# Moving small jobs from GpSimd to VectorE and SyncE inside a mixture-of-experts loop, with part of the loop unrolled

## The chip, the cores and the metric

One Trainium2 chip, one of its cores. The metric is the device time of one execution in microseconds (us); lower is better. The kernel before was run three times: 969.45, 964.38 and 969.40 us, median 969.4 us.

Engine names in the profile: PE is TensorE (PEld its weight loads), DVE is VectorE, ACT is ScalarE, POOL is GpSimd, SP is SyncE, which here only issues DMAs.

## The reference

One transformer block over x of 4 x 512 tokens and 512 channels, in float32: a modulation by a condition vector, an RWKV-style attention part (five 512 x 512 products), a channel mix (512 to 2048 and back), and then the part that matters here, a mixture of experts:

```python
probs = jax.nn.softmax(xt @ W_router, axis=-1)
top_v, top_i = jax.lax.top_k(probs, K_TOP)          # 2 of 16 experts per token
sh_mid = gelu(xt @ Wsh_up); shared_out = sh_mid @ Wsh_down
rt_mid = gelu(xt @ Wrt_up[e]);  routed_out = sum of gate * (rt_mid @ Wrt_down[e])
x = x + gb * (shared_out + routed_out)
```

Each token goes through the shared expert (512 to 512 to 512) and through two of the 16 routed experts (512 to 256 to 512).

## The kernel before, in words

Every float32 operand of a large product is split into a high and a low part, and a product is three matmuls (`mm3`, lines 417 to 421: high x high, high x low, low x high). The split of a tile is a copy (high part) and a subtraction (low part).

The order of the work of each engine is written out by hand, one program per engine, with semaphores between them. After the channel mix the kernel has these stages:

1. Shared expert for batches 0 and 1 (`shared_up`, `shared_down`, tiles of 128 tokens numbered t = 0 to 7). `gb_shared(t)` on DVE (L1737) multiplies the result in PSUM by a modulation row, into `base8[:, t]`, and raises `s_gsh`. Its PSUM banks are used again by the routed experts.
2. Scatter of the tokens to expert order in HBM (`xs_s`, by GpSimd's indirect DMA), with a table that says which expert each tile of 128 rows belongs to.
3. The expert loop: 41 tiles here, two per iteration (`pair`), in a hardware loop over `pairs` on each of PE, DVE, ACT and SP. Per tile: SP loads 128 rows (`load_xs`), PE transposes them (`turn_x`, L1174), ACT writes the high part of `xsT` (L2236), DVE the low part (`turned_lo`, L1841, which reads PSUM and `xsT`), PE multiplies by the expert's first matrix (`up`), ACT applies GELU (L2240), PE transposes that (`turn_m`, L1207), ACT and DVE split it (L2244, L1846), PE multiplies by the second matrix (`down`), DVE copies the result to SBUF (`y_out`, L1854), SP stores it (`store_y`).
4. The shared expert for batches 2 and 3, while GpSimd gathers the routed results and DVE combines them; then the output is stored.

Beside stage 3 GpSimd makes the weights ready: for experts 4 to 15 it loads half an expert (0.5 MB) into `stage` (`expert_load`, L2424) and splits it (`expert_split`: L2442 the high part, L2444 the low part; both read SBUF operands and write SBUF). The split weights stand in a ring of 5 slots; `expert_done` (L2427) makes GpSimd wait until PE has finished the expert that held the slot. PE waits for an expert on `s_exr` before `up` (L1189).

After the two halves of expert 4 (n = 0 and 1), GpSimd stops splitting and does other jobs (L2480 to L2486): six DMA loads of `x4` tiles (`x4_load`, L2453), the low part of the activations of batch 2 (`ht_lo(2)`, L2403, 4 subtractions of 128 x 512), eight additions `base8 + x4` (`base_add`, L2459, 128 x 512 each), and four DMA loads of the activations of batch 3 (`last_ht_load`, L2466). Then it goes on with expert 5.

PE's order around the start of stage 3 is L1161 to L1232: down tile 4 and 5, `turn_x(0)`, down tile 6, `up(0)`, `turn_x(1)`, down tile 7, `turn_m(0)`, with waits on `s_gsh` for 6, 7 and 8 in between, and then the loop.

Of the kernel before, what the change touches and what calls it, by code (L numbers as in the profile page):

```python
# [36 lines left out]
RING = 7  # L37
BASE = 2
PRE = 4
AHEAD = 2  # L40
SB = 2
ERING = RING - BASE
# [21 lines left out]
def adaln_block(nc, x_d, c_d, wmod_d, vecs_d, wtm_d, wcm_d, wrt_d, wex_d, out_d):  # L64
    top = ExitStack()
    with top:
        def sem(name):
            return top.enter_context(nc.semaphore(name))
# [258 lines left out]
        s_base = sem("s_base")  # L327
        s_gb = sem("s_gb")
        s_x4l = sem("s_x4l")
        s_x4p = sem("s_x4p")  # L330
        s_htp = sem("s_htp")
        s_sub = sem("s_sub")
        s_exp = sem("s_exp")
        s_gates = sem("s_gates")
# [124 lines left out]
        def x4_of(t):  # L459

            return x4m[:, t] if t < 2 else x4r[:, t - 2]
# [89 lines left out]
        def _(sp):  # L551
# [186 lines left out]
            def load_ht(b):  # L738
                for i in range(2):
                    sp.wait_ge(s_h5Tst[i], 32 * (b + 1))  # L740
                if b == 0:
                    sp.wait_ge(s_kk, (NB - 1) * MF + 12)
                elif b == 1:
                    sp.wait_ge(s_kvt, TT)
                else:
                    sp.wait_ge(s_up, KT)
                for k in range(KT):
                    sp.dma_start(ht_of(b)[:, 1, k].bitcast(F32), h5T_s[b, :, k, :]).then_inc(s_h5r[b % 2], 16)

# [11 lines left out]
            def load_x4(tiles):  # L761
                for t in tiles:
                    sp.wait_ge(s_x4st[t % TT], 16 * (t // TT + 1))
                    if t == 0:
                        sp.wait_ge(s_xklo, NB * KT)
                    sp.dma_start(x4_of(t), x4_s[t]).then_inc(s_x4l, 16)

            def scatters_landed(b):
# [52 lines left out]
            def load_xs(q, par, wait=None):  # L821
                tile = tile_of(q)
                if wait is not None:
                    sp.wait_ge(s_tx, wait)
                sp.dma_start(xsb[:, par], rows(xs_s, tile)).then_inc(s_xs[par], 16)
# [7 lines left out]
            load_xs(1, 1)  # L833
            load_xs(2, 0, 1)
            load_xs(3, 1, 2)
            def pair(i):
                load_xs(i * 2 + 4, 0, i * 2 + 3)
                store_y(i * 2, 0, i * 2 + 1 + AHEAD)
                load_xs(i * 2 + 5, 1, i * 2 + 4)
                store_y(i * 2 + 1, 1, i * 2 + 2 + AHEAD)  # L840

            pairs = sp.value_load(tend[0:1, NE:NE + 1], min_val=NE // 2, max_val=NS // 2)
            with sp.Fori(0, pairs) as i:
                pair(i)
            store_y(pairs * 2, 0, pairs * 2 + 1 + AHEAD)
            sp.wait_ge(s_yst[0], pairs * 16 + 32)
# [9 lines left out]
        def _(pe):  # L856
# [304 lines left out]
            shared_down(1, [0], first)  # L1161
            table_row()
            shared_down(1, [0], rest)
            shared_down(1, [1], every)
            pe.wait_ge(s_tab, 1)

            def turn_x(q, par, xs_count, free_count):

# [8 lines left out]
            def word_of(q):  # L1177

                return nc.values_load(tab[0:1, 0, bass.ds(q, 1)], engines=[mybir.EngineType.PE], min_val=0,
                                      max_val=8 * NE - 1,  # L1180
                                      skip_runtime_bounds_check_because="a word is 9 e + BASE - ERING (e // ERING), e under NE")

            def slot_of(word):

                return nc.s_assert_within(
                    word & 7, 0, RING - 1, skip_runtime_bounds_check_because="the low bits are (.. mod RING)")
# [33 lines left out]
                mm.then_inc(s_d4, 1)  # L1220

            turn_x(0, 0, 16, None)
            shared_down(1, [2], every)
            w0 = word_of(0)
            w1 = word_of(1)
            pe.wait_ge(s_gsh, SB * TT - 2)
            up(w0, slot_of(w0), 0, 1, None)
            turn_x(1, 1, 16, None)
            shared_down(1, [3], every)
            pe.wait_ge(s_gsh, SB * TT - 1)  # L1230
            turn_m(0, 0, 1, None)
            pe.wait_ge(s_gsh, SB * TT)  # L1232

            def pair(i, w0, w1):
                up(w1, slot_of(w1), 1, i * 2 + 2, i * 2 + 1)
# [29 lines left out]
        def _(dve):  # L1265
# [445 lines left out]
                    place_c(b - 1)  # L1711

            def ht_lo(b, tiles):
                if 0 in tiles:
                    dve.wait_ge(s_htlo, b * KT)
                hi, lo = (ht_of(b)[:, i] for i in range(2))
                for k in tiles:
                    dve.wait_ge(s_hthi, b * KT + k + 1)
                    dve.tensor_tensor(lo[:, k, :], lo[:, k, :].bitcast(F32), hi[:, k, :].bitcast(F32), ALU.subtract)\
                        .then_inc(s_htlo, 1)  # L1720
# [7 lines left out]
            def gb_shared(t):  # L1728
                dve.wait_ge(s_dn, t + 1)
                dve.wait_ge(s_gb, 16 * (t // TT + 1))  # L1730
                if t < TT:
                    dve.wait_ge(s_x4st[t], 16 * NB)
                if t == TT:
                    dve.wait_ge(s_rt, NT)
                    for i in range(2):
                        dve.wait_ge(s_h5Tst[i], 16 * NT // 2)
                dve.tensor_tensor(base8[:, t], dn_ps[t % 4][:, :], gb_bc[:, :], ALU.mult).then_inc(s_gsh, 1)  # L1737

            def gates_a():

# [90 lines left out]
            mid_lo(6)  # L1831
            mid_lo(7)
            table_d()
            gates_b()
            gb_shared(TT)
            gb_shared(TT + 1)


            def turned_lo(par, count):
# [17 lines left out]
            dve.sem_inc(s_yst[1], 16)  # L1857
            dve.sem_inc(s_yst[0], 16)
            turned_lo(0, 1)
            gb_shared(TT + 2)  # L1860
            turned_lo(1, 2)
            gb_shared(TT + 3)
            turned_mid_lo(0, 1)
            pairs = dve.value_load(tend[0:1, NE:NE + 1], min_val=NE // 2, max_val=NS // 2)

# [5 lines left out]
                y_out(1, i * 2 + 2, i * 16 + 16)  # L1871
                turned_mid_lo(0, i * 2 + 3)

            with dve.Fori(0, pairs) as i:
                pair(i)
            y_out(0, pairs * 2 + 1, pairs * 16 + 16)

# [12 lines left out]
            def combine_b(t):  # L1890
                b = t // TT
                if t >= SB * TT:
                    dve.wait_ge(s_gsh, t + 1)
                dve.wait_ge(s_bsl, 16 * (NT - SB * TT + NB))
                if t == 0:
                    dve.wait_ge(s_base, SB * TT)
                base = base8[:, t] if t < SB * TT else bsb[:, t - SB * TT]
                done(dve.tensor_tensor(g1b[:, t], g1b[:, t], gb2[:, b], ALU.mult))
                dve.tensor_tensor(g1b[:, t], g1b[:, t], base, ALU.add).then_inc(s_o4, 1)
# [24 lines left out]
        def _(act):  # L1924
# [239 lines left out]
                act.activation(h5T_of(t), t5_ps[:, :, :], ACT.Copy).then_inc(s_h5T, 1)  # L2164

            def ht_hi(b, tiles=range(KT)):
                if b == NB - 1:
                    act.wait_ge(s_htp, 64)
                    act.wait_ge(s_end, 2)
                else:  # L2170
                    act.wait_ge(s_h5r[b % 2], 64 * (b // 2 + 1))
                for k in tiles:
                    act.activation(ht_of(b)[:, 0, k, :], ht_of(b)[:, 1, k, :].bitcast(F32), ACT.Copy)\
                        .then_inc(s_hthi, 1)
# [109 lines left out]
        def _(pool):  # L2284
# [110 lines left out]


            def ht_lo(b, tiles=range(KT)):
                if b:
                    pool.wait_ge(s_htlo, b * KT)
                for k in tiles:  # L2400
                    n = b * KT + k
                    pool.wait_ge(s_hthi, n + 1)
                    pool.tensor_tensor(ht[:, 1, k, :], ht[:, 1, k, :].bitcast(F32), ht[:, 0, k, :].bitcast(F32),  # L2403
                                       ALU.subtract).then_inc(s_htlo, 1)
# [41 lines left out]
                    pool.wait_ge(s_exd, 2 * n + 2)  # L2446
                    pool.sem_inc(s_exr, 8)

            def x4_load(t):
                pool.wait_ge(s_x4st[t % TT], 16 * (t // TT + 1))  # L2450
                if t == 2:
                    pool.wait_ge(s_dn, SB * TT)
                pool.dma_start(x4_of(t), x4_s[t]).then_inc(s_x4p, 16)  # L2453

            def base_add(t):
                pool.wait_ge(s_gsh, t + 1)
                pool.wait_ge(s_x4l, 16 * 2)
                pool.wait_ge(s_x4p, 16 * (SB * TT - 2))
                pool.tensor_tensor(base8[:, t], base8[:, t], x4_of(t), ALU.add).then_inc(s_base, 1)  # L2459

            def last_ht_load():
                pool.wait_ge(s_base, SB * TT)
                for i in range(2):
                    pool.wait_ge(s_h5Tst[i], 16 * NT // 2)
                for k in range(KT):
                    pool.dma_start(ht_of(NB - 1)[:, 1, k].bitcast(F32), h5T_s[NB - 1, :, k, :])\  # L2466
                        .then_inc(s_htp, 16)

            halves = 2 * (NE - PRE)
            pool.wait_ge(s_wlo, 38)  # L2470
            expert_load(0)
# [4 lines left out]
            for n in range(halves):  # L2476
                expert_split(n)
                if n + 2 < halves:
                    expert_load(n + 2)
                if n == 1:  # L2480
                    for t in range(2, SB * TT):
                        x4_load(t)
                    ht_lo(2)
                    for t in range(SB * TT):
                        base_add(t)
                    last_ht_load()  # L2486

                if n == 16:
                    pool.wait_ge(s_gates, 1)
                    for b in range(NB):  # L2490
                        pool.dma_start(gb2[:, b], mod_s[5, b:b + 1, :].partition_broadcast(P)).then_inc(s_bsl, 16)
# [57 lines left out]
```

## Time and profile before

| what | value |
|---|---|
| median of three executions | 969.4 us |
| the profiled execution's own time | 969.45 us |
| its span (first to last instruction) | 967.7 us |
| PE busy | 896.3 us, 93% |
| DVE busy | 537.9 us, 56% |
| POOL busy | 399.2 us, 41% |
| stage 3 (from the first `up` of the loop to the last `down`) | about 747.6 to 908 us |

The shares are averages over stages with different limits. The profile's views used here are the page itself, the timeline of single engines in a stretch, tables of stretches, the listing of a tile, and the chain that ended last.

### The profile page before, as it was taken

To read this page: it belongs to the slowest core of one execution; us is meant where nothing else is said; L and a number is where in the kernel's file an instruction comes from. 1 tells how busy PE (TensorE), PEld (TensorE's weight loads), DVE (VectorE), ACT (ScalarE), POOL (GpSimd) and SP (SyncE) were. 2 spreads that over 40 slices of the span, in tenths; PEclk is the share of its full clock that TensorE was granted. 3 is DMA by queue.
4 is the path that set the end of the run, shared out by engine and by line. 5 is a ranking of instruction groups with operands and counts; after the bars stand their busy time and mean duration, and the time that the engine had idled before them with its cause. 6 is when DMAs were issued, how large, how long until landed. Compare 5 with 4: busy or idle time off the path is not lost.

```text
span 967.7 us, 13687 instructions
## 1 busy us (share of the span) xinstructions
PE 896.3 (93%) x4264; PEld 722.9 (75%) x4265; DVE 537.9 (56%) x983; ACT 383.8 (40%) x632; POOL 399.2 (41%) x314
## 2 busy tenths in 40 slices
PE   7898879999998999999999899989997999989993
PEld 2457658878776788887888788878876888878782
DVE  5896998987657111355144514451772444444488
ACT  2566455573735542321232122225441333333441
POOL 2322200100022437236104600469337989889273
PEclk9898979999998999999999999999999999999997
DMA  9549477566054536144115301564545777786686
GB/s 358 181 132 278 143 226 253 163 197 205 1 186 146 168 99 202 49 157 148 44 54 172 122 33 55 191 226 159 164 144 152 231 239 232 236 264 201 210 262 206
DMA packets 106720, 166.69 MB, mean 172 GB/s; under 512 B 8344, under 2 KB 53400, under 8 KB 105136
## 3 DMA queue, kind: packets, MB, share of 16 engines
q1 hardware_dynamic: 59184, 112.07, 34.4%
q0 software_dynamic: 10336, 35.13, 11.5%
q10 hardware_dynamic: 37152, 18.88, 6.6%
q8 instruction: 27, 0.44, 0.2%
q14 instruction: 21, 0.17, 0.1%
HBM read 98.63 MB, written 67.42 MB: 172 GB/s over the span
## 4 chain that ended last, share of the span: by engine, by line
PE 60%; POOL 14%; DVE 13%; issue 5%; DMA 4%; ACT 3%; POOLq 1%; SPq 0%; DVEq 0%; ACTq 0%
PE kv_ps L419 6%; PE kv_ps L421 6%; PE kv_ps L420 6%; PE kk_ps L419 6%; PE kk_ps L421 6%; PE kk_ps L420 6%; POOL ex_w L2444 5%; PE mm_ps L419 4%; PE mm_ps L420 4%; PE mm_ps L421 4%; POOL ex_w L2442 4%; DVE raw_ps L1352 2%; PE up_ps L419 2%; PE mm_ps L860 1%; DVE mix L1358 1%
## 5 line engine op out<-in xcount | busy, mean ns | idle before, releaser
L1552 DVE TENSOR_TENSOR silu<-kk_ps,silu 128x512 fp32r<-128x512 f32 x64 | 44.3, 692 | 205.2 <-ACT silu L2155 204.9
L2151 ACT ACTIVATE kk_ps<-kk_ps 128x512 f32<-128x512 f32 x64 | 37.2, 582 | 210.4 <-PE kk_ps L421 210.3
L419 PE MATMUL kk_ps<-xk,cm_w 128*128 128x512 f32 x256 | 101.0, 394 | 0.4 <-DVE silu L1552 0.4
L419 PE MATMUL kv_ps<-cm_w,silu 128*128 128x512 f32 x256 | 100.6, 393 | 0.0
L421 PE MATMUL kk_ps<-xk,cm_w 128*128 128x512 f32 x256 | 99.8, 390 | 0.0
L421 PE MATMUL kv_ps<-cm_w,silu 128*128 128x512 f32 x256 | 99.7, 390 | 0.0
L420 PE MATMUL kk_ps<-xk,cm_w 128*128 128x512 f32 x256 | 99.7, 389 | 0.0
L420 PE MATMUL kv_ps<-cm_w,silu 128*128 128x512 f32 x256 | 99.6, 389 | 0.0
L2327 POOL TENSOR_TENSOR rs<-mv,neghalf 128x4 f32<-128x4 f32 x12 | 13.6, 1133 | 162.7 <-DVE mv L1281 162.6
L1841 DVE TENSOR_TENSOR xsT<-xs_ps,xsT 128x512 fp32r<-128x512 f32 x42 | 29.1, 692 | 90.9 <-ACT xsT L2236 90.9
L2320 POOL TENSOR_TENSOR cm_w<-stage,cm_w 128x1024 fp32r<-128x1024 f32 x16 | 38.7, 2425 | 91.8 <-ACT cm_w L1942 91.8
L2372 POOL TENSOR_TENSOR rs<-mv,neghalf 128x1 f32<-128x1 f32 x16 | 16.2, 1015 | 137.6 <-DVE mv L1577 137.6
L1970 ACT ACTIVATE mix<-raw_ps 128x512 fp32r<-128x512 f32 x64 | 37.4, 596 | 64.0 <-DVE raw_ps L1352 57.6
L419 PE MATMUL mm_ps<-mix,wkv_w 128*128 128x512 f32 x128 | 54.7, 428 | 7.9 <-DVE x2b L1391 4.4
L419 PE MATMUL up_ps<-ex_w,xsT 128*128 x164 | 50.2, 306 | 9.4 <-issue 6.2
L2444 POOL TENSOR_TENSOR ex_w<-stage,ex_w 128x1024 fp32r<-128x1024 f32 x24 | 57.4, 2390 | 1.9
L419 PEld LDWEIGHTS kk_ps<-xk,cm_w 128*128 128x128 f32 x256 | 48.1, 188 | 10.6 <-DVE silu L1552 0.8
L421 PEld LDWEIGHTS kk_ps<-xk,cm_w 128*128 128x128 f32 x256 | 48.1, 188 | 10.2
L421 PEld LDWEIGHTS kv_ps<-cm_w,silu 128*128 128x128 f32 x256 | 48.0, 188 | 10.1
L420 PEld LDWEIGHTS kv_ps<-cm_w,silu 128*128 128x128 f32 x256 | 48.1, 188 | 9.8
L419 PEld LDWEIGHTS kv_ps<-cm_w,silu 128*128 128x128 f32 x256 | 48.1, 188 | 9.8
L420 PEld LDWEIGHTS kk_ps<-xk,cm_w 128*128 128x128 f32 x256 | 48.1, 188 | 9.6
(275 smaller groups left out, 2368.4 us busy)
## 6 DMA issues: line engine op xcount, KB each, us to landing
xs_s<-zero ACTq DMA_DIRECT2D x13, 1024.0 KB, 6.0
stage<-in_wex POOLq DMA_DIRECT2D x24, 512.0 KB, 5.0
xsb<-xs_s SPq DMA_DIRECT2D x44, 256.0 KB, 3.5
ys_s<-ysb SPq DMA_DIRECT2D x41, 256.0 KB, 2.8
stage<-in_wcm SPq DMA_DIRECT2D x16, 512.0 KB, 3.8
wmod<-in_wmod SPq DMA_DIRECT2D x6, 1024.0 KB, 11.7
ex_raw<-in_wex SPq DMA_DIRECT2D x6, 1024.0 KB, 7.5
stage<-in_wtm SPq DMA_DIRECT2D x10, 512.0 KB, 6.2
```

The source lines that it names most:

```text
L419: pe.matmul(out, lhs[0], rhs[0], start=first, stop=False)
L420: pe.matmul(out, lhs[0], rhs[1], start=False, stop=False)
L421: return pe.matmul(out, lhs[1], rhs[0], start=False, stop=last)
L1352: dve.scalar_tensor_tensor(out=out, in0=dT[:, k, :], scalar=vecs[:, vec, k:k + 1], in1=hT[:, k, 0:T], op0=ALU.mult, op1=ALU.add).then_inc( ...
L1552: dve.tensor_tensor(silu[:, g % NSILU, 1, :], kk_ps[g % 2][:, :], silu[:, g % NSILU, 0, :].bitcast(F32), ALU.subtract).then_inc(s_silo, 1)
L1841: dve.tensor_tensor(xsT[:, par, 1], xs_ps[par][:, :, :], xsT[:, par, 0].bitcast(F32), ALU.subtract)\
L1970: act.activation(mix[:, i % 2, 0, k, :], raw_at(s, b, k), ACT.Copy)\
L2151: act.activation(kk_ps[g % 2][:, :], kk_ps[g % 2][:, :], ACT.Silu).then_inc(s_silu, 1)
L2320: pool.tensor_tensor(w[:, 1, k0:k0 + KT // 2, :], stage[:, n % 2].rearrange("p (k c) -> p k c", c=H), w[:, 0, k0:k0 + KT // 2, :].bitcast( ...
L2372: pool.tensor_tensor(rs5[:, t % 2:t % 2 + 1], mv5[:, t % 2, 1:2], neghalf[:, :], ALU.pow)\
L2442: pool.tensor_tensor(hi, stage[:, n % 2], zero[:, 0:1].to_broadcast([P, HALF]), ALU.add).then_inc(s_exd, 1)
L2444: pool.tensor_tensor(lo, stage[:, n % 2], hi.bitcast(F32), ALU.subtract).then_inc(s_exd, 1)
```

## The change

The four jobs leave GpSimd. The six `x4` loads and the four loads for batch 3 are issued by SP. `ht_lo(2)`, the eight `base_add` and `gates_b` (three small operations that stood before the loop) go to DVE, spread over the first seven pairs: after pair 0 and 1 two subtractions each, after pairs 2 to 5 two additions each, after pair 6 `gates_b`. For that, the first seven iterations are written out on DVE and on SP, and the hardware loop there starts at 7; PE's and ACT's loops stay as they are. On PE, down tiles 6 and 7 now stand before `turn_x(0)`, with a single wait for `s_gsh` 8.

```diff
+PEEL = 7
 # SP
                 elif b == 2:
+                    sp.wait_ge(s_up, KT)
                 else:
-                    sp.wait_ge(s_up, KT)
+                    sp.wait_ge(s_dn, SB * TT)
                 for k in range(KT):
                     sp.dma_start(ht_of(b)[:, 1, k].bitcast(F32), h5T_s[b, :, k, :]).then_inc(s_h5r[b % 2], 16)
...
+                    if t == 2:
+                        sp.wait_ge(s_dn, SB * TT)
                     sp.dma_start(x4_of(t), x4_s[t]).then_inc(s_x4l, 16)
...
             load_xs(3, 1, 2)
+            load_x4(range(2, SB * TT))
...
+            for i in range(PEEL):
+                pair(i)
+            sp.wait_ge(s_base, SB * TT)
+            load_ht(NB - 1)
             pairs = sp.value_load(tend[0:1, NE:NE + 1], min_val=NE // 2, max_val=NS // 2)
-            with sp.Fori(0, pairs) as i:
+            with sp.Fori(PEEL, pairs) as i:
 # PE
-            shared_down(1, [1], every)
+            shared_down(1, [1, 2, 3], every)
             pe.wait_ge(s_tab, 1)
+            pe.wait_ge(s_gsh, SB * TT)
...
             turn_x(0, 0, 16, None)
-            shared_down(1, [2], every)
             w0 = word_of(0)
+            up(w0, slot_of(w0), 0, 1, None)
             w1 = word_of(1)
-            pe.wait_ge(s_gsh, SB * TT - 2)
-            up(w0, slot_of(w0), 0, 1, None)
             turn_x(1, 1, 16, None)
-            shared_down(1, [3], every)
-            pe.wait_ge(s_gsh, SB * TT - 1)
             turn_m(0, 0, 1, None)
-            pe.wait_ge(s_gsh, SB * TT)
 # DVE
+            def base_add(t):
+                dve.wait_ge(s_gsh, t + 1)
+                dve.wait_ge(s_x4l, 16 * SB * TT)
+                dve.tensor_tensor(base8[:, t], base8[:, t], x4_of(t), ALU.add).then_inc(s_base, 1)
...
-            gates_b()
...
-            with dve.Fori(0, pairs) as i:
+            def beside(i):
+                if i < 2:
+                    ht_lo(2, [2 * i, 2 * i + 1])
+                elif i < 6:
+                    base_add(2 * i - 4)
+                    base_add(2 * i - 3)
+                else:
+                    gates_b()
+
+            for i in range(PEEL):
+                pair(i)
+                beside(i)
+            with dve.Fori(PEEL, pairs) as i:
                 pair(i)
 # GpSimd
-                if n == 1:
-                    for t in range(2, SB * TT):
-                        x4_load(t)
-                    ht_lo(2)
-                    for t in range(SB * TT):
-                        base_add(t)
-                    last_ht_load()
```

## Rows read from the trace of the kernel before

**Rows 1.** The page, part 4: engines' shares of the chain that ended last.
```profile
PE 60%; POOL 14%; DVE 13%; issue 5%; DMA 4%; ACT 3%; POOLq 1%; SPq 0%; DVEq 0%; ACTq 0%
```

**Rows 2.** Table of stretches: start:end, length, busy us per engine, PEclk, DMA share, GB/s.
```profile
770.00:868.00 98.00, 94.69 (x605) 80.69 (x603) 43.97 (x77) 34.24 (x75) 87.23 (x57) 1.00 0.75 242
...
752.00:757.00 5.00, 4.65 (x34) 4.11 (x33) 2.03 (x4) 1.37 (x3) 3.90 (x4) 1.00 1.01 386
```

**Rows 3.** Timeline of PE before the loop: start, length, engine, operation, [idle before].
```profile
737.26 0.63 PE L1174 MATMUL xs_ps<-ident,xsb 128*128 128x128 f32 x4 [3.06 <-DMA xsb<-xs_s]
...
740.23 0.39 PE L421 MATMUL dn_ps<-ex_w,mid 128*128 128x512 f32 x1
...
745.08 0.38 PE L1207 MATMUL tm_ps<-ident,mb 128*128 128x128 f32 x2
747.60 0.38 PE L419 MATMUL up_ps<-ex_w,xsT 128*128 x1 [2.13 <-issue]
```

**Rows 4.** Timeline of DVE there: `gb_shared` of tiles 6 and 7.
```profile
740.66 0.69 DVE L1737 TENSOR_TENSOR base<-dn_ps,gb_bc 128x512 f32<-128x512 f32 x1 [1.41 <-PE dn_ps L421]
...
745.28 0.69 DVE L1737 TENSOR_TENSOR base<-dn_ps,gb_bc 128x512 f32<-128x512 f32 x1 [1.43 <-PE dn_ps L421]
```

**Rows 5.** PE's waits from 748 to 904 us; its timeline, and POOL's, at the longest.
```profile
PE up_ps L419 <- POOLq L2447: 2.3, 1, 2.3
...
870.38 0.38 PE L419 MATMUL up_ps<-ex_w,xsT 128*128 x1 [2.34 <-POOLq L2447]
...
867.55 2.34 POOL L2444 TENSOR_TENSOR ex_w<-stage,ex_w 128x1024 fp32r<-128x1024 f32 x1
```

**Rows 6.** Timeline of POOL: the jobs that move, experts 5 and 15.
```profile
747.64 3.23 POOL L2453 DMA_DIRECT2D x4r<-x_s  x6
...
770.13 1.89 POOL L2442 TENSOR_TENSOR ex_w<-stage,zero 128x1024 fp32r<-128x1024 f32 x1 [0.21 <-issue]
...
881.94 1.90 POOL L2442 TENSOR_TENSOR ex_w<-stage,zero 128x1024 fp32r<-128x1024 f32 x1
```

**Rows 7.** One pair's turn: DVE's and PE's timelines, L1841's durations (ns, min/median/max).
```profile
755.62 0.42 DVE L1846 TENSOR_TENSOR mbT<-tm_ps,mbT 128x256 fp32r<-128x256 f32 x1
758.33 0.69 DVE L1841 TENSOR_TENSOR xsT<-xs_ps,xsT 128x512 fp32r<-128x512 f32 x1 [2.29 <-ACT xsT L2236]
...
757.06 0.60 PE L1174 MATMUL xs_ps<-ident,xsb 128*128 128x128 f32 x4
759.32 0.38 PE L419 MATMUL up_ps<-ex_w,xsT 128*128 x1
...
L1841 DVE TENSOR_TENSOR xsT<-xs_ps,xsT x39: 691/692/693, 750.4 to 900.4; 128x512 fp32r<-128x512 f32 x39
```

**Rows 8.** Earlier stage, timelines of DVE and POOL: operations side by side.
```profile
630.77 1.10 DVE L1617 TENSOR_TENSOR lg<-lg,rev 128x64 f32<-128x64 f32 x1
631.91 0.22 DVE L1618 TENSOR_REDUCE top<-lg 128x4 f32<-128x64 f32 x1
632.16 0.96 DVE L1619 TENSOR_TENSOR oh<-rev,top 128x64 f32<-128x64 f32 x1
...
684.32 2.73 DVE L1568 TENSOR_TENSOR x4b<-x4b,ub 128x512 f32<-128x512 f32 x1
689.51 0.69 DVE L1568 TENSOR_TENSOR x4b<-x4b,ub 128x512 f32<-128x512 f32 x1
...
630.50 1.29 POOL L2353 TENSOR_TENSOR x4b<-x4b,bc 128x512 f32<-128x512 f32 x1 [0.74 <-DMA h5b<-in_x]
631.75 1.29 POOL L2354 TENSOR_TENSOR ub<-ub,bc 128x512 f32<-128x512 f32 x1
...
681.76 4.75 POOL L2314 TENSOR_TENSOR ex_w<-ex_raw,ex_w 128x1024 fp32r<-128x1024 f32 x2 [3.92 <-ACT ex_w L1931]
```

**Rows 9.** SP's DMA issues, and issue to landing of `xsb` (748 to 904 us).
```profile
700.73 2.56 SPq L748 DMA_DIRECT2D ht<-h5T_s  x4
...
DMA to landing us min/median/max: 2.5/3.3/6.7
```

More of the change, by code:

```diff
@@ L329, in adaln_block @@
         s_x4l = sem("s_x4l")
-        s_x4p = sem("s_x4p")
-        s_htp = sem("s_htp")
         s_sub = sem("s_sub")
@@ L744, in load_ht @@
                     sp.wait_ge(s_kvt, TT)
+                elif b == 2:
+                    sp.wait_ge(s_up, KT)
                 else:
-                    sp.wait_ge(s_up, KT)
+                    sp.wait_ge(s_dn, SB * TT)
                 for k in range(KT):
@@ L1713, in ht_lo @@
             def ht_lo(b, tiles):
-                if 0 in tiles:
-                    dve.wait_ge(s_htlo, b * KT)
+                if b == 1 and 0 in tiles:
+                    dve.wait_ge(s_htlo, KT)
                 hi, lo = (ht_of(b)[:, i] for i in range(2))
@@ L1833, in _ @@
             table_d()
-            gates_b()
-            gb_shared(TT)
-            gb_shared(TT + 1)
+            for t in range(TT, SB * TT):
+                gb_shared(t)
             def turned_lo(par, count):
@@ L1859, in _ @@
             turned_lo(0, 1)
-            gb_shared(TT + 2)
             turned_lo(1, 2)
-            gb_shared(TT + 3)
             turned_mid_lo(0, 1)
@@ L1894, in combine_b @@
                 dve.wait_ge(s_bsl, 16 * (NT - SB * TT + NB))
-                if t == 0:
-                    dve.wait_ge(s_base, SB * TT)
                 base = base8[:, t] if t < SB * TT else bsb[:, t - SB * TT]
@@ L2166, in ht_hi @@
             def ht_hi(b, tiles=range(KT)):
+                act.wait_ge(s_h5r[b % 2], 64 * (b // 2 + 1))
                 if b == NB - 1:
-                    act.wait_ge(s_htp, 64)
                     act.wait_ge(s_end, 2)
-                else:
-                    act.wait_ge(s_h5r[b % 2], 64 * (b // 2 + 1))
                 for k in tiles:
@@ L2397, in ht_lo @@
             def ht_lo(b, tiles=range(KT)):
-                if b:
-                    pool.wait_ge(s_htlo, b * KT)
                 for k in tiles:
@@ L2447, in expert_split @@
                     pool.sem_inc(s_exr, 8)
[L2449 to L2467, printed above, removed]
             halves = 2 * (NE - PRE)
```

## The prediction

> **What bounds the kernel now.** I read the page's chain first [rows 1]: PE holds 60% of it and POOL 14%. The reader is to see that POOL is on the chain at all, since it computes nothing of the output directly; most of its share lies in the expert loop. So next comes the table of stretches over the loop [rows 2]: between 770 and 868 us PE is busy 94.69 of 98 us and POOL 87.23 of 98. Both run close to full, PE a little more. Then PE's waits in the loop [rows 5]: one of 2.34 us at 870.38, released by POOL's count of finished experts, because the second half of that expert's split began at 867.55 and took 2.34 us. Last the hand-over into the loop: PE waits 3.06 us for the first rows [rows 3], and stands 2.13 us idle before the `up` at 747.60. A tile of the loop takes PE (870.38 - 2.34 - 747.60) / 31 = 3.89 us [rows 3, 5]: from the `up` of tile 1 to that of tile 32 are 31 tiles. (Tile 0's `up` stands before the loop; an iteration begins with the `up` of an odd tile, and the stalled one is in the middle of the sixteenth.) A pair is 7.77 us.
>
> The profiled execution took 969.45 us, 1.75 more than its span, and is the upper one of the three, 0.05 above the median of 969.4. I sum against it.
>
> **Part 1, POOL freed.** POOL leaves splitting at 747.64 and comes back at 770.13 [rows 6]: 22.5 us for 6 DMA issues, 12 tensor operations and 4 DMA issues. All go. Not all 22.5 us are gained: expert 5 takes the slot of expert 0, so its split waits until PE has finished expert 0, which has two or three tiles (41 tiles over 16 experts). The last `down` of tile q ends about 3.4 us after the `up` of tile q+1 (3.89 less the half microsecond of `turn_m`), so with the loop entered at 746.6 (below) expert 0 is done at about 754 or 758, and POOL is 12 to 16 us earlier than 770.13. From there it needs (881.94 - 770.13) / 10 = 11.2 us per expert [rows 6] against PE's 3.89 x 41 / 16 = 10.0, so it falls back about 1.2 us per expert, as before, and reaches expert 13 still 12 us early or more. The stall of 2.34 us goes. What is late next is nothing of POOL's: later experts had no wait before either. Term: -2.34, bounds 0 and -2.34.
>
> **Part 2, the hand-over.** Before, two `down` tiles lie behind `turn_x(0)`. Now they fill the 3.06 us in which PE waited for the first rows. PE is free at 737.26 - 3.06 = 734.20. A tile is 12 matmuls, about 2.75 us, so both are done at about 739.7. The new wait for all eight of `s_gsh` stands before `turn_x(0)`: DVE multiplies tile 7 in 0.69 us [rows 4], it started 0.04 us after the last matmul of tile 6 ended (740.23 + 0.39), so about 740.45, and PE starts `turn_x(0)` at about 740.6. Behind that wait is the whole of PE's queue and through it ACT, DVE and SP's loads. From a `turn_x` to the next `up` over ACT and DVE are 759.32 - 757.06 = 2.26 us [rows 7]: `up(0)` at 742.9, itself 3.89 - 2.26 = 1.6 us, `turn_x(1)` at 744.5. Now this chain is exposed a second time, with nothing but `turn_m(0)` under it: `up(1)` at 744.5 + 2.1 = 746.6. Before it was 747.60. There, PE's last wait ended with DVE's multiply at 745.28 + 0.69 = 745.97 [rows 4], so entering the loop took it 1.6 us; now `turn_m(0)` can go at about 745.1 and the entry ends by 746.7, so both ways agree. Term: -1.0. Bounds: a gain of 2.1 (all the idle before 747.60), a loss of 0.5 (the reads of expert words that stood under a `down` tile are now bare).
>
> **Part 3, the work put on DVE.** By time alone it is free. At a pair's end DVE stands idle 2.29 us before the next L1841 [rows 7], and two operations of 128 x 512 take about 1.3 us (0.69 each, the second starting a little into the first). But L1841 has hardly any room behind it: it ends at 759.02 and PE's `up` starts at 759.32. A DVE that comes out of its extra work more than about 2.3 us after the pair's end holds PE, microsecond for microsecond.
>
> The rows that matter are from another stage [rows 8]. L1617 (both inputs in SBUF, 128 x 64) took 1.10 us, while the single-input L1618 beside it took 0.22. POOL was in an operation from 630.50 to 631.79, and L1617 ended at 631.87, just after it. L1619, again two SBUF inputs, came at 632.16 into the next POOL operation (631.75 to 633.04) and ended at 633.12. In the wide form it is the same: L1568 took 2.73 us at 684.32, where the identical one at 689.51 took 0.69; POOL was in two splits from 681.76 to 686.51. So a DVE operation with two SBUF inputs waits for POOL's running operation to end. L1841 never does: 39 of it at 691 to 693 ns with POOL busy nine tenths of the time [rows 7, 2]; one of its inputs is PSUM. The operations that the change brings into the loop, `ht_lo` and `base_add`, have both inputs in SBUF, and on POOL they could not meet a split, since they ran in its own order.
>
> The Trainium skill says the same as a rule, against this change ("SBUF — State Buffer", on the engines' shared port pair): a VectorE instruction with two SBUF inputs contends with a GpSimd instruction that reads SBUF, and whichever comes second is blocked for the whole of the first. By the rule the price is the one below, while a reader who goes by durations alone would put this part at zero; the trace agrees with the rule, 2.73 us against 0.69.
>
> The price: half an expert is one POOL operation of 1.9 us, one of 2.35 us directly after it, and about 1.3 us of idle and issuing (5.6 in all). The first DVE operation falls into the 1.9 (34%): it waits 0.95 on average, runs 0.69, then POOL's next is first in line for 2.35, then the second DVE operation 0.69; together 4.7, which is 2.4 over the 2.3 that are free. Into the 2.35 (42%): the wait is up to 2.35 and then both run, 1.3 to 3.7, on average 0.4 over. Into the rest (24%): half of the time the second operation meets the next 1.9, 0.9 over. Mean 0.34 x 2.4 + 0.42 x 0.4 + 0.24 x 0.45 = 1.1 us per pair. Pairs 0 to 5 have two such operations each; at the end of pair 0, about 755, POOL may still wait for expert 0. Five pairs give 5.4. Bounds: 0, and 6 x 3.3 = 20 for the worst phase each time. I take +5.4, since the rows show blocking wherever such operations met. `gates_b` after pair 6 has one operation of the kind, a small one: +0.2 (0 to 1). POOL is held by the same lock, 0.7 us each time, which its lead of 12 us hides.
>
> **Part 4, the work put on SP.** Ten issues move into SP's queue. At 700.73 four took 2.56 us [rows 9], 0.64 each. The six `x4` loads, behind `load_xs(3)` at about 745.2, take 3.8 us and push `load_xs(4)` from about 748.9 to 749.9; it is needed by `turn_x(4)`, 757.06 before, 756.0 now, and landing takes 3.3 us, at most 6.7 [rows 9]. That maximum is this very load, when the same 1.5 MB came from POOL's queue and the DMA engines were full, 386 GB/s at share 1.01 [rows 2]. The bytes are the same and come 2 us sooner, so I expect no stall. Behind pair 6, SP does four loads (2.56), a register read and the loop's entry, then `load_xs(18)`: some 3 us late, with 4 us of room at the median landing and 1 MB queued ahead: +0.3. Together 0 to 3; I take +0.3. Landing of the batch 3 data itself is not late: it is needed after 910.
>
> Gone from the hand-over are also `gates_b` on DVE (under PE's tile 5, worth nothing). The stage after the loop waits for the last store and shifts as a whole.
>
> **Sum.** 969.45 - 2.34 - 1.0 + 5.4 + 0.2 + 0.3 = 972.0 us, 2.6 over the median before.
>
> **Rivals.** (a) The blocking costs nothing, because the operations fall into POOL's idle parts or PE's own waits cover it: 969.45 - 3.3 + 0.3 = 966.4. For it: POOL is idle or issuing a quarter of the time, and at pair 0 perhaps waiting. Against: rows 8, and six chances. (b) The other side, slower than before: the pair's end falls into POOL's 1.9 us operation in most pairs, 2.4 us each. POOL's half of 5.6 and the pair of 7.8 drift against each other, but a PE that is held moves with POOL. Five at 2.4 make 12 instead of 5.4: about 979. It shows as slower from a total of 8.2 us of blocking on (3.3 gained, 4.9 of tolerance). (c) SP's bursts: `turn_x(4)` and `turn_x(18)` wait 1 to 3 us for their rows, together 3 more than in my sum: 975. For it, the landing of 6.7 us with only about 0.5 to spare; against it, no wait for rows in the whole loop before. (d) The stall moves instead of vanishing would give 974.3, but needs 12 us of lead lost; I give it nothing of its own.
>
> **How the numbers follow.** Main case 0.52, (a) 0.22, (b) 0.13, (c) 0.13. Within 0.5% (4.9 us either way, about what a measurement of this kernel tells from no change; one of its three runs was 5 us below the others) lie 0.38 of the main case, whose own range is 968 to 978, 0.14 of (a) and 0.06 of (c): 0.58. Slower: 0.13 + 0.13 + 0.07 = 0.33 (main above 974.3, all of (b), half of (c)). Faster: the rest of (a) with a low draw like 964.38, 0.08, and a little for unknown gains, 0.09. The range 965 to 979 leaves out the low draws and the far end of (b).
>
> **What would show it.** PE's wait for L2447 gone, and POOL's expert 5 beginning at 754 to 758; the `up` of tile 1 at 746.6. L1719 and the new additions in the loop with maxima of 2.5 to 3 us instead of 0.69, and PE idle before the middle `up` of pairs 1 to 6, 0 to 3 us each, released by DVE's `xsT`. If these operations last 0.69 throughout, part 3 is wrong and (a) holds. If PE waits for `xsb`, (c). If POOL begins expert 5 later than 760, part 1's lead was smaller than I think.

## The result, and the profile after

The changed kernel took 974.6 us (median of 13 executions, 969.33 to 978.12), the kernel before 965.4 us (13, 963.05 to 970.13): ratio 1.0093, 95% interval [1.0077, 1.0110]. That is 9 us slower. Forecast were 972.0 us and a range of 965 to 979. The time lies inside, but the difference is the better measure: forecast +2.6 us over a before of 969.45, measured +9.2 between the medians. "Slower by over 0.5%" had a chance of 0.33 only. The profiled execution took 973.85 us, span 972.1 us, 4.4 over the span of before.

From the page of the changed kernel, the share of the chain that ended last, against [rows 1]:

```profile
PE 74%; DVE 15%; issue 4%; DMA 3%; ACT 2%; SPq 1%; DVEq 0%; ACTq 0%
```

POOL is gone from it, and yet the kernel is slower. Freeing an engine on the chain is worth only what PE waited for it, 2.34 us [rows 5]. The table of stretches, the first line against [rows 2]:

```profile
770.00:868.00 98.00, 90.80 (x569) 77.52 (x568) 54.47 (x83) 32.46 (x71) 82.78 (x53) 0.98 0.72 234
752.00:757.00 5.00, 4.81 (x33) 4.13 (x32) 3.77 (x5) 2.29 (x5) 2.94 (x2) 1.00 0.51 163
736.00:742.00 6.00, 3.38 (x17) 3.13 (x17) 1.38 (x2) 0.60 (x1) 5.60 (x4) 0.71 0.41 130
742.00:748.00 6.00, 4.62 (x22) 4.20 (x21) 1.02 (x2) 1.41 (x4) 1.42 (x2) 0.50 0.58 172
784.00:790.00 6.00, 3.96 (x19) 3.91 (x19) 2.68 (x4) 1.08 (x3) 5.44 (x4) 0.72 0.51 165
```

PE lost 3.9 us of work in the first stretch, and the granted clock (the third number from the end) is below 1.00 in the last three; the kernel before had 1.00 in all of them. PE's timeline in the loop, each row a first matmul of `up` with the idle time before it (the last row, tile 32, has none):

```profile
760.11 0.38 PE L418 MATMUL up_ps<-ex_w,xsT 128*128 x1 [2.06 <-issue]
...
764.04 0.38 PE L418 MATMUL up_ps<-ex_w,xsT 128*128 x1 [0.19 <-issue]
...
776.30 0.38 PE L418 MATMUL up_ps<-ex_w,xsT 128*128 x1 [0.73 <-issue]
...
786.05 0.39 PE L418 MATMUL up_ps<-ex_w,xsT 128*128 x1 [2.04 <-issue]
...
874.73 0.38 PE L418 MATMUL up_ps<-ex_w,xsT 128*128 x1
```

The 0.19 us is what every iteration's entry costs. The other three, with a second 0.73 at 803.70, stand after pairs 0, 2, 3 and 5: 5.56 us. The wait for POOL, 2.34 us at the same tile in [rows 5], has gone (last row). DVE's timeline names the cause of the four (operations that last too long), and POOL's beside it shows what they waited for. The two engines hold each other up; below this is called the lock. DVE first, then POOL:

```profile
754.90 4.31 DVE L1726 TENSOR_TENSOR ht<-ht 128x512 fp32r<-128x512 f32 x2
759.13 0.68 DVE L1852 TENSOR_TENSOR xsT<-xs_ps,xsT 128x512 fp32r<-128x512 f32 x1
...
764.64 1.28 DVE L1726 TENSOR_TENSOR ht<-ht 128x512 fp32r<-128x512 f32 x2
...
772.42 2.98 DVE L1749 TENSOR_TENSOR base<-base,x4m 128x512 f32<-128x512 f32 x2
...
780.84 4.31 DVE L1749 TENSOR_TENSOR base<-base,x4r 128x512 f32<-128x512 f32 x2
785.08 0.68 DVE L1852 TENSOR_TENSOR xsT<-xs_ps,xsT 128x512 fp32r<-128x512 f32 x1
...
792.15 1.28 DVE L1749 TENSOR_TENSOR base<-base,x4r 128x512 f32<-128x512 f32 x2
```

```profile
753.98 1.88 POOL L2458 TENSOR_TENSOR ex_w<-stage,zero 128x1024 fp32r<-128x1024 f32 x1 [9.97 <-PE dn_ps L420]
755.94 2.72 POOL L2460 TENSOR_TENSOR ex_w<-stage,ex_w 128x1024 fp32r<-128x1024 f32 x1
...
761.52 2.40 POOL L2460 TENSOR_TENSOR ex_w<-stage,ex_w 128x1024 fp32r<-128x1024 f32 x1
764.52 0.57 POOL L2440 DMA_DIRECT2D stage<-in_wex  x1 [0.60 <-POOL ex_w L2460]
767.67 1.88 POOL L2458 TENSOR_TENSOR ex_w<-stage,zero 128x1024 fp32r<-128x1024 f32 x1 [2.58 <-PE dn_ps L420]
...
772.91 1.94 POOL L2458 TENSOR_TENSOR ex_w<-stage,zero 128x1024 fp32r<-128x1024 f32 x1
774.93 2.71 POOL L2460 TENSOR_TENSOR ex_w<-stage,ex_w 128x1024 fp32r<-128x1024 f32 x1
...
790.43 0.57 POOL L2440 DMA_DIRECT2D stage<-in_wex  x1 [0.59 <-POOL ex_w L2460]
795.10 1.88 POOL L2458 TENSOR_TENSOR ex_w<-stage,zero 128x1024 fp32r<-128x1024 f32 x1 [4.10 <-PE dn_ps L420]
```

Two operations take 1.28 us when POOL stands still (at 764.64, where POOL issues a DMA and waits until 767.67; at 792.15, where it waits until 795.10) and 4.31 when they begin in one POOL operation and meet the next. At 754.90 the first waits until 755.86, the end of POOL's first operation, and runs. POOL's next is held by it (2.72 instead of 2.40), and the second DVE operation waits until 758.66. Then `xsT` starts at 759.13 and PE's `up` at 760.11, 2.06 us late. The 2.98 us at 772.42 (and 3.00 at 799.80) are the case between: the first operation begins just before POOL's and is through in 0.68, only the second waits, until 774.85, and PE loses 0.73. DVE's idle time does not show this; a reader of the totals sees an engine busy 57% of the span. The profile books PE's idle time to "issue", not to `xsT`; only the two timelines side by side show it.

The hand-over, against [rows 3] and [rows 4], on PE:

```profile
736.88 0.63 PE L1186 MATMUL xs_ps<-ident,xsb 128*128 128x128 f32 x4 [0.83 <-issue]
739.30 0.57 PE L418 MATMUL up_ps<-ex_w,xsT 128*128 x1 [1.79 <-DVE xsT L1852]
...
742.02 1.06 PE L1186 MATMUL xs_ps<-ident,xsb 128*128 128x128 f32 x4
742.87 0.63 PE L1219 MATMUL tm_ps<-ident,mb 128*128 128x128 f32 x2
744.88 0.58 PE L418 MATMUL up_ps<-ex_w,xsT 128*128 x1 [1.38 <-DVE xsT L1852]
...
747.61 1.05 PE L1186 MATMUL xs_ps<-ident,xsb 128*128 128x128 f32 x4
```

From an `up` to the next `turn_x` are 2.7 us here, and 1.5 before (`turn_x(2)` at 749.12, the `up` of [rows 3] at 747.60). `turn_x` itself shows 1.05 for 0.60. That is the clock of 0.50, the lower of its two levels (1.2 GHz).

To compare stretches I count from one event to another, since the profiles reach the expert table's transpose (`t_ps`) at different times; the differences before it, 3.6 us between these two, are in code that the change leaves alone. "Tile n" is the start of `turn_x(n)`:

| us | table to tile 2 | tile 2 to 18 | tile 18 to 41 | tile 41 to the end | sum |
|---|---|---|---|---|---|
| before | 18.9 | 62.2 | 91.6 | 64.8 | 237.5 |
| changed | 21.0 | 70.5 | 89.2 | 64.8 | 245.5 |

### The profile page after: what moved, and what is told of

Its sections match the earlier page's. It is cut to its first block, busy times and chain, and to the rows that moved or that the text cites. A ratio compares the mean times of both kernels' runs of the same rounds, so it can differ in the third digit from the quotient of the medians.

```text
span 972.1 us, 13587 instructions
## 1 busy us (share of the span) xinstructions
PE 897.2 (92%) x4264; PEld 724.7 (75%) x4265; DVE 553.9 (57%) x995; ACT 383.8 (39%) x632; POOL 379.7 (39%) x292
## 4 chain that ended last, share of the span: by engine, by line
PE 74%; DVE 15%; issue 4%; DMA 3%; ACT 2%; SPq 1%; DVEq 0%; ACTq 0%
PE kv_ps L418 6%; PE kk_ps L418 6%; PE kv_ps L420 6%; PE kk_ps L419 6%; PE kv_ps L419 6%; PE kk_ps L420 6%; PE mm_ps L418 4%; PE mm_ps L420 4%; PE mm_ps L419 4%; PE up_ps L418 4%; PE up_ps L419 3%; PE up_ps L420 3%; PE dn_ps L418 3%; PE dn_ps L420 3%; PE dn_ps L419 3%
```

## The experiments

In all variants PE's wait `s_exr >= word + 1` reads `(word & 127) + 1`, which has the same value and costs one register operation per tile. The variant c0_before measures that operation alone. There are three groups, each on a chip of its own with its own runs of before: e1 to e4 (before 970.35), then c1, e5 to e7 (973.06), then c0, c2, e8 (965.1). Ratios are to before unless said.

**e1_hand_back**: the changed kernel with the order of PE and DVE at the hand-over as before.

```diff
-            shared_down(1, [1, 2, 3], every)
+            shared_down(1, [1], every)
...
             turn_x(0, 0, 16, None)
+            shared_down(1, [2], every)
...
             turn_x(1, 1, 16, None)
+            shared_down(1, [3], every)
...
```

> The changed kernel with the hand-over into the loop put back as before on PE and DVE (down tiles 6 and 7 behind turn_x(0) and turn_x(1), the additions and loads stay on DVE and SP). Theory: of the 8.0 us that the loop's stretch grew, 2.1 lie before turn_x(2) and 0.45 in the tile after it at the lower clock; putting the order back takes them away: 974.6 - 2.5 = about 972. The granted clock should be 1.00 from 736 to 748 us, and the up of tile 1 take 1.5 us. Rival (my prediction's step): the new order was worth 1.0 us, so this gives about 975.6.

Measured 978.1 us, ratio 1.0071 [1.0044, 1.0097]. The same four stalls, at the same tiles: 2.06, 0.73, 2.06 and the small last. They do not hang on the hand-over. In its profile the clock is 1.00 from 736 to 748 and the table to tile 2 takes 18.2 us, as the theory has it. Its ratio is 3.5 us below that of c1_after and c2_after (1.0107 each), but those ran on other chips and the intervals overlap, so the gain of 2.5 us is not shown.

**e2_hand_only**: the kernel before with only that order new.

```diff
-            shared_down(1, [1], every)
+            shared_down(1, [1, 2, 3], every)
...
```

> The kernel before with nothing changed but that order on PE and DVE. Theory: turn_x(2) comes 2.5 us later, but PE then also comes later to expert 13, where it stood 2.3 us for GpSimd, so the loss is swallowed there: 965.4 + 0.2 = 965.6, with PE's wait for GpSimd near 0 and PEclk below 1.00 before the loop. Rival 1 (my prediction's step): a gain of 1.0, and the wait at expert 13 grows by it, so 965.4 too, but with turn_x(2) earlier. Rival 2: both add up, 968.

Measured 971.45 us, 1.0010 [0.9992, 1.0028]. The clock stayed at 1.00, and the table to tile 2 took 18.05 us, 0.8 less than before. PE then waits longer for POOL:

```profile
PE up_ps L419 <- POOLq L2443: 7.0, 3, 3.1
```

PE goes into the loop earlier and POOL does not, so what the hand-over gives comes back as waits for weights: 7.0 us in three, where before had 2.3. The wait did not fall to nothing, as the theory had it; rival 1 had its direction.

**e3_one_input**: the changed kernel, the twelve operations replaced by statistics of one 128 x 512 input (same length, one SBUF input; the sums and low parts are left out, so the output is not the reference's).

```diff
...
-                dve.tensor_tensor(base8[:, t], base8[:, t], x4_of(t), ALU.add).then_inc(s_base, 1)
+                dve.bn_stats(scrap[:, t], base8[:, t]).then_inc(s_base, 1)
```

> The changed kernel in which the four subtractions of batch 2 and the eight additions on DVE are replaced by statistics operations over the same 128 x 512 tile (one SBUF input, 0.69 us each in the trace of before); these results are left out. Theory (two SBUF inputs wait for GpSimd's running operation): each lasts 0.69, PE's idle before the middle up of pairs 1 to 6 goes, 5.4 us and 1.4 us of lower clock behind one of them: 974.6 - 6.8 = about 968. Rival (DVE's time, its waits or the written-out loop itself hold PE): 974.6, no change.

Measured 975.1 us, 1.0059 [1.0035, 1.0084]. From the grouped lines of DVE in the loop (line, operation, count, busy us, mean ns):

```profile
L1856 DVE TENSOR_TENSOR xsT<-xs_ps,xsT 128x512 fp32r<-128x512 f32 x39 | 27.0, 691 | 71.9 <-ACT xsT L2258 71.9
...
L1753 DVE BATCH_NORM_STATS2 scrap<-base 128x6 f32<-128x512 f32 x8 | 5.1, 680 | 0.0
L1766 DVE TENSOR_TENSOR gates<-pr,gates 128x16 f32<-128x16 f32 x1 | 2.0, 2030 | 0.0
```

680 ns, with POOL splitting as before: not one is held, while `gates_b`'s two-input operation over 128 x 16 took 2.03 us. All stalls in pairs 0 to 5 are gone (tile 2 to 18: 63.7 us instead of 70.5). So the lock is the second SBUF input, not DVE's time. Nor is it what they write, though the statistics write 6 columns and not 512: `xsT` writes 512 beside POOL and takes 0.691 us, with one input in PSUM, and `gates_b`, which writes 16, is held. The times do not show the gain. The profiled execution, 967.01 us, was the fastest of this variant's eight, and the median is 8 us above it; against e1_hand_back, which has the four stalls (and the old hand-over) and ran on the same chip, the mean is 2.4 us lower (e1 to e3 1.0025 [0.999, 1.006]). Where the other executions lost the 8 us, one profile does not tell.

**e4_loads_only**: the kernel before with only the ten DMA issues moved to SP.

```diff
+            load_x4(range(2, SB * TT))
...
+            sp.wait_ge(s_base, SB * TT)
+            load_ht(NB - 1)
```

> The kernel before in which only the ten DMA issues leave GpSimd for SP, placed as in the changed kernel; all arithmetic and the hand-over stay. Theory: GpSimd is about 7 us earlier at expert 5, the wait of 2.3 us at expert 13 goes, turn_x(18) waits about 1 us for its rows behind the four loads: 965.4 - 1.3 = 964.1. Rival: SP's bursts cost as much as the wait, 965.4 or more.

Measured 973.2 us, 1.0030 [1.0014, 1.0046], which is c0_before's ratio (below), so the ten issues by themselves are worth nothing that can be told; the forecast gain of 1.3 us did not come. The stall of expert 13 is gone, `turn_x(18)` is 1.0 us late, as in the changed kernel. The order of the hand-over is the old one, and yet the clock is 0.79 from 730 to 736 in its profile.

**c1_after**: the changed kernel, with the register operation.

> The changed kernel itself, once more, on the chip of the three others (only PE's wait for an expert takes its number from the low seven bits of the word, one register operation more per tile, as in all of these variants). It gives the base for them. Theory: ratio to before 1.009, the same four waits of PE in pairs 0, 2, 3 and 5 adding to 5.6 us, since the order of the engines is fixed. Whether PE's granted clock falls to 0.50 at 739 us again is open: if that fall comes from the new order, it must be there again and the tiles 1 and 2 take about 5 us each; if it is chance, the clock stands at 1.00 there in about half of the profiles and the hand-over is 2 to 3 us shorter.

Measured 983.4 us, 1.0107 [1.0082, 1.0131]. Stalls 1.98, 0.74 and two more at the same tiles. The clock stood at 1.00 throughout the hand-over:

```profile
742.88 0.38 PE L418 MATMUL up_ps<-ex_w,xsT 128*128 x1 [1.70 <-DVE xsT L1852]
...
746.82 0.38 PE L418 MATMUL up_ps<-ex_w,xsT 128*128 x1 [1.34 <-DVE xsT L1852]
```

The idle times before both `up` are nearly those of the changed kernel (1.79 and 1.38), and the `up` of tile 1 comes 16.5 us after the table instead of 18.2 (before: 17.4). So the clock does not follow from the new order: the same instructions met it at 1.00 here.

**e5_fill**: PE's idle time at the hand-over filled with transposes.

```diff
+            fill(5)
             turn_x(0, 0, 16, None)
+            fill(11)
...
             turn_m(0, 0, 1, None)
+            fill(8)
```

> The changed kernel with transposes of a constant put into PE's idle time before and behind turn_x(0) and behind turn_m(0) (5, 11 and 8 of 128 x 128, 0.15 us each, into unused columns of a PSUM bank; nothing reads them). Theory: the +2.1 us of the hand-over come from the lower granted clock after PE's idle time; with PE busy the clock stays at 1.00, up(0) and up(1) take 1.5 us instead of 2.9, and the time is 2 to 3 us below the changed kernel's (ratio to it 0.997). Rival 1, the reads of the expert words and the bare chain are the cost: nothing changes or the filler's own length adds 0.5 us. Rival 2, the clock falls by chance: it may fall here as well, at another place.

Measured 982.3 us, 1.0084 [1.0054, 1.0113]; against c1_after by the means of their runs 0.9986 [0.996, 1.001]. The clock stayed at 1.00, as it did in c1_after without filling, and the hand-over was 0.6 us longer (18.7). Whether filling helps in those executions in which the clock falls is not settled by this.

**e6_spread**: the changed kernel with one of the twelve operations after each half pair, instead of two after each pair.

```diff
                 turned_mid_lo(1, i * 2 + 2)
+                if between is not None:
+                    beside(between)
...
+            def beside(j):
+                if j < 4:
+                    ht_lo(2, [j])
+                elif j < 12:
+                    base_add(j - 4)
...
+                pair(i, 2 * i)
+                beside(2 * i + 1)
```

> The changed kernel with the twelve moved operations of DVE one by one, after every half pair, in place of two after each pair (same operations, same inputs, same count). Theory (blocking by POOL's running operation): a single operation waits at most 2.35 us and takes 0.69, which is 0.8 over the 2.2 us that are free, and mostly under it; so PE's waits of 5.6 us in pairs 0, 2, 3 and 5 fall to about 0.6 and the time is 5 us below the changed kernel's (ratio to before 1.004). Rival, that POOL's port blocks in any case and the cost goes with the number of such operations: 5.6 us stay. Rival, that the unrolled code or DVE's mere occupancy costs: the same 5.6 stay.

Measured 976.3 us, 1.0044 [1.0024, 1.0065]; against c1_after, on the same chip, 0.9938 [0.992, 0.996], 6 us, where 5 were forecast. The operations are still held, but singly (DVE's timeline; the third row is the `xsT` that PE waits for, the last is `gates_b`):

```profile
769.25 0.68 DVE L1749 TENSOR_TENSOR base<-base,x4m 128x512 f32<-128x512 f32 x1
...
773.19 1.84 DVE L1749 TENSOR_TENSOR base<-base,x4r 128x512 f32<-128x512 f32 x1
775.24 0.69 DVE L1852 TENSOR_TENSOR xsT<-xs_ps,xsT 128x512 fp32r<-128x512 f32 x1 [0.20 <-ACT xsT L2254]
...
800.92 2.38 DVE L1762 TENSOR_TENSOR gates<-pr,gates 128x16 f32<-128x16 f32 x1
```

The longest of the twelve leaves 0.20 us before `xsT`, and none of them makes a tile late. `gates_b` does: its 2.38 us, behind two short operations, run past the gap, and the `up` of tile 16 comes 0.84 us late, in e7_all_three too (0.1 in the changed kernel, 0.5 in e3). This variant is therefore not free of the lock. Same operations, same number, same lock: what cost was two in a row in a gap of 2.2 us.

**e7_all_three**: e6 with the hand-over of before and batch 3's loads one per pair.

```diff
-            for i in range(PEEL):
+            for i in range(PEEL + 3):
                 pair(i)
-            sp.wait_ge(s_base, SB * TT)
-            load_ht(NB - 1)
+                if i == PEEL - 1:
+                    sp.wait_ge(s_base, SB * TT)
+                if i >= PEEL - 1:
+                    load_ht(NB - 1, [i - PEEL + 1])
...
```

> Operations one by one as in the spread variant, the hand-over of PE and DVE of the kernel before, and the four loads for batch 3 one per pair after pairs 6 to 9 in place of four after pair 6. Theory: against before the expert 13 stall of 2.3 us goes, 0.6 of blocking comes, turn_x(18) no longer waits (1.0), the hand-over is as before: 1.7 us below before, ratio 0.998. Rival, that SP's loads or the unrolled code cost more than is seen in the loop's rows: 2 to 3 us over before as in the variant that only moves the loads (1.003).

Measured 975.2 us, 1.0016 [0.9996, 1.0036]. `turn_x(18)` has no wait (3.94 us after tile 17; 5.20 in e6). Against c1_after 0.992 [0.990, 0.994]. It was forecast below before (0.998) and is not. In its profile the clock is 0.71 from 730 to 736 and 0.72 from 736 to 742, with the old order.

**c0_before**, **c2_after**: both kernels with nothing but the register operation, on one chip.

```diff
-                pe.wait_ge(s_exr, word + 1)
+                pe.wait_ge(s_exr, (word & 127) + 1)
```

> The kernel before itself, with nothing but the one register operation of PE per tile that all variants have. It tells what that operation does by itself. In every variant's profile PE stands idle for instructions ('issue') 2.7 to 9 us in all between 925 and 940 us, in the last stage, where the kernel before and the changed kernel show none. Theory: these gaps belong to where PE's code lies in memory (that operation moves it), so they are here too, the stage after the loop takes 67 to 73 us instead of 64.8 and the ratio to before is 1.003 to 1.007; all other variants are then to be read against this one. Rival: the gaps come from SP's moved loads and the unrolled code; then this variant shows 64.8 and a ratio of 1.000.

> The changed kernel with the same one operation, as a pair with the variant above on the same chip. Ratio of the two by the loop's rows: 5.6 of blocking + 1.0 of turn_x(18) - 2.3 (stall of expert 13) = +4.3 us, and -0.8 from the hand-over where the clock stays at 1.00 or +2.1 where it falls: 3.5 to 6.4 us, 1.004 to 1.007.

Measured c0_before 968.1 us, 1.0032 [1.0016, 1.0048]; c2_after 975.5 us, 1.0107 [1.0083, 1.0130]. Their ratio by the means is 1.0075 [1.005, 1.010], 7 us, a little over the forecast of 1.004 to 1.007. My theory of c0_before fell: its last stage took 64.9 us without a gap. So did the rival, since its ratio is not 1. The gaps are no matter of the kernel: c1_after and c2_after are the same program, and between 927 and 939 us PE shows

```profile
927.00:939.00 12.00, 8.61 (x28) 5.81 (x29) 8.06 (x12) 1.82 (x3) 7.33 (x7) 0.89 0.90 288
```

in the first and

```profile
927.00:939.00 12.00, 12.00 (x55) 9.93 (x54) 9.28 (x14) 2.73 (x4) 8.80 (x9) 1.00 0.91 260
```

in the second. All eight profiles of the first two groups have such gaps (0.3 to 1.75 us each), none of the third, and the kernel before was 5 to 8 us slower in those two groups. Ratios within a group are the safe reading; the last stage (64.8 to 73.6 us over the profiles) is left out of comparisons. Where the register operation costs its 3 us I did not find: c0_before's profile has the tile times of before, but it is that of its fastest execution (964.12 us, 4 below its median), so it cannot show the loss.

c0_before has no stall at expert 13 either. POOL began its first split 4.0 us behind the table there, and 6.6 in before (731.67 and 736.86), so its `x4` loads began at 742.46, 5.2 us earlier than in [rows 6], while PE's tile 2 was only 3.2 earlier. The 2.34 us hang on how early POOL is at the table, and may be missing in executions of before too; there is only one profile of before to tell.

**e8_dve_only**: the kernel before with only the twelve operations on DVE, one per half pair; all loads stay on GpSimd.

```diff
...
                 if n == 1:
                     for t in range(2, SB * TT):
                         x4_load(t)
-                    ht_lo(2)
-                    for t in range(SB * TT):
-                        base_add(t)
+                if n == 13:
                     last_ht_load()
```

> The kernel before with only the twelve subtractions and additions moved to DVE, one after each half pair of the first six pairs; all ten DMA loads stay with GpSimd (the four of batch 3 after expert 10), the hand-over and gates_b as before. Theory: no blocking that PE sees (0.0 to 0.6, as in the spread variant), no wait of turn_x(18), no stall at expert 13 (-2.3): 2 us below the same-code before (ratio to that 0.998), the lowest of all. Rival, that the moved work costs time even one by one: not below it.

Measured 966.2 us, 1.0014 [0.9994, 1.0033]; against c0_before 0.9987 [0.997, 1.000]. The lowest variant but not one that beats the kernel before by more than can be told. In its profile the clock is 0.74 from 744 to 750, behind the 2.29 us in which PE is idle before the loop (tile 3 is 1.25 us late), and `turn_x(18)` waited 0.5 for its rows though no SP load stands before it; I had put both at nothing.

## Why the prediction was right in part and wrong in its difference

- **Part 1 (-2.34): right in the profile, but worth less in the mean.** POOL's expert 5 began at 753.98 (forecast 754 to 758), and the stall went: tile 33 came 3.78 us after tile 32 instead of 6.10. But c0_before's one profile has no such stall, so a part of before's executions may have had nothing to give; how many is open. The sum took one execution's stall for the kernel's.
- **Part 2 (-1.0): the step that failed.** In the profile the hand-over is 2.1 us longer. The working was right as long as PE has its full clock: c1_after put the `up` of tile 1 at 16.5 us behind the table, 0.85 less than before. But that -1.0 was the gain over one execution too: with the old order that `up` came at 16.6 to 16.7 us in e1, c0 and e8, where PE waited 2.1 to 2.2 us for its first rows and not 3.06, and against those the new order gains 0.1 to 0.2. What the term did not price is the clock. It had both bare stretches of the chain (PE is idle for 0.83 + 1.79 and for 1.38 us in them), but not that what follows may run at half the clock: two `up` of 1.5 us became 2.7. In the profiles with the new order this happened to both `up` in the changed kernel, to the first alone in c2_after, e3 and e6 (tile 1 after 5.05 us instead of 3.86), to none in c1_after, e2 and e5. It also happened with the old order, in e4 and e7, but not in before, e1 and c0, where PE was idle for 2.1 to 3.1 us ahead of `turn_x(0)`. So both orders run this risk, and against before's one execution the new one was worth anything from -0.85 to +2.1. What it is worth in the mean is not shown: e2, which has only this change, is 2 us below c0_before by their ratios, e1 points the other way, and both comparisons cross chips.
- **Part 3 (+5.4, and 0.2 for `gates_b`): right in mechanism, place and size.** 5.56 us of PE's idle time. My forecast had five pairs at 1.1 on average; it was four, at 2.06, 0.73, 2.04 and 0.73, with two free ones, where POOL, now ahead, stood waiting for a slot. "POOL is freed" and "DVE is blocked by POOL" work against each other there. e3 shows that the second SBUF input is the cause, e6 that the pair of operations is. Held up in its turn, POOL lost 0.3 us each time (2.72 for 2.40), not the 0.7 that I gave it. What I left out is again the clock: after the stall at 786.05 it was 0.72, and tiles 11 and 12 lost 1.4 us beyond the wait. The same stood behind that stall in e1 and e5, behind both long stalls in c2_after, and behind neither in c1_after (clock 1.00). Tiles 5, 9, 11, 12 and 15 together are 6.9 us late; e6 against c1_after gives 6 us for the whole part on the chip. `gates_b` took 1.66 us at its two-input operation and tile 17 was 0.1 late (0.84 in e6 and e7, inside its bounds).
- **Part 4 (+0.3): too small.** `turn_x(4)` had no wait, as forecast. `turn_x(18)` waited 0.85 us and tile 18 was 1.0 late, here and, by 1.0 to 1.6, in e1, e3, e4, e5, e6 and both copies of the changed kernel; in e7, with the four loads spread, it was not. SP's rows there, then PE's:

```profile
808.66 1.81 SPq L749 DMA_DIRECT2D mid<-h5T_s  x4
812.05 0.34 SPq L828 DMA_DIRECT2D xsb<-xs_s  x1
```

```profile
818.06 0.66 PE L1186 MATMUL xs_ps<-ident,xsb 128*128 128x128 f32 x4 [0.85 <-DMA xsb<-xs_s]
```

  The load went out at 812.05 and the rows were used 6.0 us later, where I had reckoned with a landing of 3.3 at the median and 1 MB ahead at no price.
- **The sum.** By the two profiles, from the table on: +2.1 (part 2), +6.9 and 0.1 (part 3), +1.0 (part 4), -2.3 (part 1), and +0.45 for tile 3, still at the low clock: 8.2, against 8.0 in the table above. The forecast of 972.0 is close to 974.6 in part because it started from 969.45, an execution 4 us above the median of the 13. Of the rivals, (a) is refuted; (b) has the right total in the medians (9) but not its cause, since blocking was 5.6 to 7 us; (c) is right for a third of its price.

What the change costs, then: 9 us plain, 7 us between c0_before and c2_after. By e6 against c1_after 6 us are part 3, on another chip; the row sum of 6.9 agrees, while e3's times, whose profile has the stalls gone, do not show the gain. Why the plain pair differs by 2 us more than the other, within their intervals, stays open, and with it what the register operation does.

## What to carry to other kernels

Before an operation moves from GpSimd to VectorE, look at its inputs: with two in SBUF it waited here for GpSimd's running operation, and beside GpSimd operations of 1.9 and 2.4 us all twelve fitted singly into gaps of 2.2 us (the longest took 1.84), while pairs of them did not fit four times of six, and `gates_b` behind two short operations did not either. Place them singly, right behind what the next engine waits for. A gap that is safe at any phase is one foreign operation plus its own, by an estimate from these rows about 3.1 us (2.4 + 0.69); the gaps here were shorter and held by where the two engines happened to stand. An idle stretch that a reordering leaves bare on TensorE should be priced twice, once without and once with a half clock behind it, and a stall seen in one profile of before should be looked for in a second one before it is counted as a gain.

## What was not expected of the hardware

- The clock at the hand-over differs between executions of the same program: at 1.00 throughout in c1_after, at 0.71 and 0.50 in two stretches of 6 us in the changed kernel, 0.72 from 738 to 744 in c2_after. It fell behind idle time each time, but the same idle time (0.83 and 1.70 us) was followed by either level. The Trainium skill ("TensorE: Matmul & The Clock Gate", Part 1) says that the number of slow matmuls at a kernel's start varies between runs of one kernel; these rows show the same in its middle.
- The kernel with one register operation more per tile on PE took 0.3% longer (1.0032 [1.0016, 1.0048]), and no row of its profile, taken of its fastest execution, shows where.
- PE can stand without instructions for up to 1.75 us at a time in the last stage, in every profile of two groups of runs and in none of a third, with the same program (c1_after and c2_after, 71.8 and 64.9 us for that stage). The cause is not known.
- The lock works both ways, and the two engines take turns: behind POOL's operation came one of DVE's, then POOL's next (2.72 us for 2.40, the wait counted in), then DVE's second. The Trainium skill ("SBUF — State Buffer", on the shared port pair) has the loser wait for the whole instruction. DVE's side agrees, 4.31 us for two operations that take 1.28 undisturbed; POOL's grew by 0.32 only, less than the 0.68 that one such operation takes.
